# Gated cross-attention and feed-forward block: who squares the key tiles

## The chip, the cores and the metric

The kernel runs on one core of a Trainium2 chip. A core has a matrix engine (TensorE), a vector engine (VectorE), an engine for activations (ScalarE), a programmable engine (GpSimd) and one that issues transfers (SyncE). Each works through its own list of instructions in order; they wait for each other by semaphores. The metric is the device time of one execution in microseconds (us), the median of several runs.

## What is computed

The inputs are 16 batches of 512 tokens with 512 channels, a context of 120 tokens for each batch, positions, a mask and the weights. Two gated steps follow one another.

```
x = x + tanh(g_xattn) * attention(layernorm(x), ctx)     # 16 heads of 32, e / (1 + sum e), bias by distance
x = x + tanh(g_ffn)   * ffn(layernorm(x))

def ffn(x):
    xr = mu_r * x + (1 - mu_r) * x_prev                  # x_prev: the token before
    xk = mu_k * x + (1 - mu_k) * x_prev
    r  = sigmoid(xr @ W_r)
    k_act = square(relu(xk @ W_k))
    return r * (k_act @ W_v)
```

The change touches `square` in the `k_act` line.

## The kernel before

The kernel goes through the 16 batches in a loop. The attention of batch b is interleaved with the feed-forward of batch b-1, so the loop body `batch(b, ffn, last)` exists once on every engine, and in it each engine's order is written out by hand. Batch 0 has no feed-forward beside it; the batches 1 to 15 have, and the feed-forward of the last batch runs in a tail with code of its own (`tail_relu`, `tail_square`, `tail_high`, `tail_low`). Products are made to full precision by splitting each operand into a high and a low part (fp32r) and multiplying three times: high by high, high by low, low by high. Four channel tiles by three passes make 12 matmuls of 128x512 for a product.

The attention goes by token tiles t = 0 to 3 and groups of four heads g = 0 to 3. For each tile TensorE makes the scores (L589), VectorE adds the bias (L1188) and takes the row maxima (L1194), ScalarE makes the exponentials of 16 heads (`exps`, L884), VectorE the reciprocals of the sums (L1207, L1209), GpSimd normalises half a tile at a time (`normalise_probs`, L1496), TensorE transposes by groups (L683) into two banks in turn, ScalarE copies them out (`probs_out`, L891), TensorE multiplies by the values (L694), ScalarE and VectorE split the result (`attn_out` L898, `attn_low` L1213), and TensorE projects it.

The feed-forward's key step goes by channel tiles m = 0 to 3. TensorE makes a key product in one of two rotating banks. ScalarE takes it with a Relu into `relu` (`relu_out`, L932), GpSimd squares `relu` into `square` (`squares`, L1533), ScalarE rounds `square` to the high part of `xt_or_act` (`act_split`, L936), and GpSimd subtracts to get the low part (`squares_low`, L1537). `relu` and `square` are single buffers: the Relu of tile m+1 waits until square m is made (`square_ready`), and the square of tile m+1 until low part m is made (`act_low`). The first value product reads `xt_or_act` channel tile by channel tile and waits for each low part (`act_low`). Tiles 0 to 3 are worked on while the attention's tiles 0 and 1 go through softmax. Both buffers also serve as scratch for the mixing step of the odd token tiles (`diffs`, `mix_ks`), which comes later in the batch.

Of the kernel before, what the change touches and what calls it, by code (L numbers as in the profile page):

```python
# [10 lines left out]
ALU = mybir.AluOpType  # L11
ACT = mybir.ActivationFunctionType
# [31 lines left out]
def flamingo_block(nc, x, x_t, ctx_t, qpos, kpos, mask, g_xattn, g_ffn, wq, wk, wv, wo,  # L44
# [6 lines left out]
    CT = D // P  # L51
# [19 lines left out]
    with ExitStack() as stack:  # L71
        def sb(name, shape, dt=F32):
            return stack.enter_context(nc.sbuf_tensor(name, shape, dt))

        def sem(name):
            return stack.enter_context(nc.semaphore(name))
# [35 lines left out]
        relu = sb("relu", [P, S])  # L112
        square = sb("square", [P, S])
# [91 lines left out]
        read = {k: sem(f"{k}_read") for k in ("key", "gate", "value", "proj", "query", "turn2")}  # L205
# [44 lines left out]
        square_ready = sem("square_ready")  # L250
        act_high = sem("act_high")
        act_low = sem("act_low")
# [580 lines left out]
        def _(act):  # L833
# [45 lines left out]
            def exps(b, t, g):  # L879

                act.wait_ge(max_ready, (b * QT + t) * G + g + 1)
                for j in range(J):
                    head = g * J + j
                    e = act.activation(probs[:, t % 2, head, :], probs[:, t % 2, head, :], ACT.Exp,  # L884
                                       bias=neg_max[:, t % 2, head:head + 1],
                                       accum_out=sums[:, t % 2, head:head + 1])
                e.then_inc(exp_done, 1)
# [37 lines left out]
            def relu_out(b, m):  # L925
# [5 lines left out]
                    act.wait_ge(square_ready, b * CT + m)  # L931
                act.activation(relu[:], bank_of["key", m][:], ACT.Relu).then_inc(read["key"], 1)  # L932

            def act_split(b, m):
                act.wait_ge(square_ready, b * CT + m + 1)
                act.copy(xt_or_act[:, HI, m, :], square[:]).then_inc(act_high, 1)  # L936
# [27 lines left out]
            def batch(b, ffn, last):  # L964
                f = b - 1

                def feed_forward(*steps):
                    for step, n in steps:
                        if ffn:
                            step(f, n)  # L970
                        elif (step, n) in late:
                            late_out(late[step, n])

                def after(*steps):
                    if not last:
                        for step, n in steps:
                            step(b + 1, n)

                late = {(gate_out, n): LATE_USES.index(("gate", n)) for n in range(QT)}
                late.update({(relu_out, n): LATE_USES.index(("key", n)) for n in range(CT)})  # L980
                feed_forward((gate_out, 0))
                exps(b, 0, 0)
                exps(b, 0, 1)
                feed_forward((gate_out, 1))
                exps(b, 0, 2)
                exps(b, 0, 3)
                feed_forward((relu_out, 0))
                probs_out(b, 0, 0)
                probs_out(b, 0, 1)
                exps(b, 1, 0)  # L990
                feed_forward((act_split, 0), (relu_out, 1))
                exps(b, 1, 1)
                probs_out(b, 0, 2)
                probs_out(b, 0, 3)
                exps(b, 1, 2)
                feed_forward((act_split, 1))
                attn_out(b, 0)
                feed_forward((relu_out, 2))
                exps(b, 1, 3)
                feed_forward((act_split, 2))  # L1000
                exps(b, 2, 0)
                probs_out(b, 1, 0)
                probs_out(b, 1, 1)
                feed_forward((relu_out, 3))
                probs_out(b, 1, 2)
                probs_out(b, 1, 3)
                feed_forward((act_split, 3))
                exps(b, 2, 1)
                exps(b, 2, 2)
                attn_out(b, 1)  # L1010
                exps(b, 2, 3)
                after((split_x_high, 0))
                probs_out(b, 2, 0)
                after((split_x_high, 1))
                exps(b, 3, 0)
                exps(b, 3, 1)
                probs_out(b, 2, 1)
                probs_out(b, 2, 2)
                probs_out(b, 2, 3)
                feed_forward((gate_out, 2))  # L1020
                turn2_out(b, 0)
                attn_out(b, 2)
                exps(b, 3, 2)
                exps(b, 3, 3)
                probs_out(b, 3, 0)
                probs_out(b, 3, 1)
                after((split_x_high, 2))
                probs_out(b, 3, 2)
                probs_out(b, 3, 3)
                turn2_out(b, 1)  # L1030
                mix_key_high(b, 0)
                attn_out(b, 3)
                feed_forward((gate_out, 3))
                mix_gate_high(b, 0)
                after((split_x_high, 3))
                if not ffn:

                    act.wait_ge(late_done, len(LATE_USES))
                    weight(5)
                mix_key_high(b, 1)  # L1040
                if not last:
                    turn2_out(b, 2)
                    mix_gate_high(b, 1)
                    mix_key_high(b, 2)
                    turn2_out(b, 3)
                    mix_key_high(b, 3)
                    mix_gate_high(b, 2)
                else:
                    mix_gate_high(b, 1)
                    turn2_out(b, 2)  # L1050
                    mix_key_high(b, 2)
                    mix_gate_high(b, 2)
                    gate_out(b, 0, tail_bank)
                    turn2_out(b, 3)
                    gate_out(b, 1, tail_bank)
                    mix_key_high(b, 3)
                mix_gate_high(b, 3)
# [35 lines left out]
            with act.Fori(1, NB - 1) as b:  # L1093
                batch(b, True, False)
# [365 lines left out]
        def _(pool):  # L1460
# [65 lines left out]
                pool.tensor_tensor(mixed_gate[:, LO, :, tokens], diffs[t % 2][:], as_f32(mixed_gate[:, HI, :, tokens]),  # L1526
                                   ALU.subtract).then_inc(mixg_low, 1)

            def squares(b, m):
                pool.wait_ge(read["key"], b * CT + m + 1)  # L1530
                if m > 0:
                    pool.wait_ge(act_low, b * CT + m)
                pool.tensor_tensor(square[:], relu[:], relu[:], ALU.mult).then_inc(square_ready, 1)  # L1533

            def squares_low(b, m):
                pool.wait_ge(act_high, b * CT + m + 1)
                pool.tensor_tensor(xt_or_act[:, LO, m, :], square[:], as_f32(xt_or_act[:, HI, m, :]),  # L1537
# [2 lines left out]
            def batch(b, ffn, last):  # L1540
                f = b - 1

                def feed_forward(*steps):
                    if ffn:
                        for step, n in steps:
                            step(f, n)

                def after(*steps):
                    if not last:
                        for step, n in steps:  # L1550
                            if n is None:
                                step(b + 1)
                            else:
                                step(b + 1, n)

                normalise_probs(b, 0, 0)
                feed_forward((squares, 0))
                normalise_probs(b, 0, 1)
                feed_forward((squares_low, 0), (squares, 1))
                normalise_probs(b, 1, 0)  # L1560
                feed_forward((squares_low, 1), (squares, 2))
                normalise_probs(b, 1, 1)
                feed_forward((squares_low, 2), (squares, 3), (squares_low, 3))
                rstd2_of(b, 0)
                normalise_probs(b, 2, 0)
                normalise_probs(b, 2, 1)
                after((split_x_low, 0))
                normalise_probs(b, 3, 0)
                edge(b, 0)
                difference(b, 0)  # L1570
                rstd2_of(b, 1)
                normalise_probs(b, 3, 1)
                after((split_x_low, 1), (split_x_low, 2))
                edge(b, 1)
                rstd2_of(b, 2)
                after((rstd1_of, None))
                difference(b, 1)
                after((split_x_low, 3))
                if last:
                    mix_low(b, 0)  # L1580
                    mix_low(b, 1)
                edge(b, 2)
                if not last:
                    mix_low(b, 0)
                rstd2_of(b, 3)
                if not last:
                    mix_low(b, 1)
                difference(b, 2)
                edge(b, 3)
                difference(b, 3)  # L1590
                mix_low(b, 2)
                mix_low(b, 3)
# [35 lines left out]
```

## Time and profile before

| | us |
|---|---|
| median of 3 runs | 1287.36 |
| lowest, highest | 1286.8, 1287.39 |
| the profiled execution | 1286.61 |
| its span on the core | 1284.8 |
| TensorE busy | 1271.9 |
| VectorE busy | 1048.6 |
| ScalarE busy | 836.7 |
| GpSimd busy | 782.2 |

The span is what the profile's rows cover; the rest of the execution lies around it. Busy times count instructions that run, not waits. The granted clock of TensorE is at its full level throughout. In rows of the timeline the first number is the start in us from the span's start and the second the time from the start of the first to the end of the last of the instructions merged in the row; on ScalarE an instruction may start while the one before it is ending. Brackets at a row's end give idle time before it and the engine that ended it. PE is TensorE's matmul, PEld its weight load, DVE is VectorE, ACT ScalarE and POOL GpSimd.

### The profile page before, as it was taken

To read this page: it belongs to the slowest core of one execution; us is meant where nothing else is said; L and a number is where in the kernel's file an instruction comes from. 1 tells how busy PE (TensorE), PEld (TensorE's weight loads), DVE (VectorE), ACT (ScalarE), POOL (GpSimd) and SP (SyncE) were. 2 spreads that over 40 slices of the span, in tenths; PEclk is the share of its full clock that TensorE was granted. 3 is DMA by queue.
4 is the path that set the end of the run, shared out by engine and by line. 5 is a ranking of instruction groups with operands and counts; after the bars stand their busy time and mean duration, and the time that the engine had idled before them with its cause. 6 is when DMAs were issued, how large, how long until landed. Compare 5 with 4: busy or idle time off the path is not lost.

```text
span 1284.8 us, 30825 instructions
## 1 busy us (share of the span) xinstructions
PE 1271.9 (99%) x9848; PEld 1044.9 (81%) x9848; DVE 1048.6 (82%) x2834; ACT 836.7 (65%) x2868; POOL 782.2 (61%) x731
## 2 busy tenths in 40 slices
PE   8999999999999999999999999999999999999998
PEld 7888788888878888888888888888888888888887
DVE  4767797988978788888978798897879888798885
ACT  5457494875848395674939477584848667493952
POOL 0014666666666676676676766666676666676651
PEclk9999999999999999999999999999999999999999
DMA  9772314032231304123130402213140312312000
GB/s 286 211 230 73 114 36 131 8 78 86 58 98 57 106 8 116 48 59 105 50 105 24 139 8 70 94 50 105 48 115 8 100 64 59 105 50 56 10 26 33
DMA packets 75377, 103.74 MB, mean 81 GB/s; under 512 B 26960, under 2 KB 33104, under 8 KB 75344
## 3 DMA queue, kind: packets, MB, share of 16 engines
q1 hardware_dynamic: 75344, 103.31, 26.9%
q8 instruction: 19, 0.31, 0.1%
q14 instruction: 14, 0.11, 0.0%
HBM read 78.62 MB, written 24.67 MB: 80 GB/s over the span
## 4 chain that ended last, share of the span: by engine, by line
PE 97%; DVE 1%; issue 1%; POOL 0%; ACT 0%; DMA 0%; DVEq 0%; ACTq 0%; POOLq 0%
PE rotating L510 71%; PE score_bank L589 5%; PE attn_bank L694 5%; PE probs_bank L683 5%; PE attn_bank L683 4%; PE score_bank L510 4%; PE score_bank L605 2%; PE probs_bank L605 0%; DVE w_value L1132 0%; DMA probs<-in_ctx_t_dram 0%; PE probs_bank L510 0%; PE attn_bank L510 0%; DVE mix_k L1252 0%; DVE square L1252 0%; PE attn_bank L551 0%
## 5 line engine op out<-in xcount | busy, mean ns | idle before, releaser
L884 ACT ACTIVATE probs<-probs,neg_max 128x120 f32<-128x120 f32 x1024 | 390.7, 386 | 8.0 <-DVE neg_max L1194 7.0
L1496 POOL TENSOR_TENSOR probs<-probs,recip 128x960 f32<-128x960 f32 x128 | 232.5, 1816 | 177.4 <-DVE recip L1209 177.4
L1188 DVE SCALAR_TENSOR_TENSOR probs<-mask_in,score_bank 128x120 f32<-128x120 f32 x1024 | 213.7, 271 | 24.0 <-PE score_bank L589 23.9
L884 ACT ACTIVATION_READ_ACCUMULATOR probs<-probs,neg_max 128x1 f32 x1024 | 195.3, 191 | 0.0
L510 PE MATMUL rotating<-w_gate,mixed_gate 128*128 128x512 f32 x756 | 190.9, 398 | 3.2 <-DVE query_t L1173 2.5
L510 PE MATMUL rotating<-w_proj,attn_t 128*128 128x512 f32 x768 | 191.5, 398 | 0.0
L510 PE MATMUL rotating<-w_value,xt_or_act 128*128 128x512 f32 x720 | 180.1, 399 | 0.0
L510 PE MATMUL rotating<-mixed_key,w_key 128*128 128x512 f32 x720 | 178.2, 396 | 0.0
L510 PE MATMUL rotating<-xt_or_act,w_query 128*128 128x512 f32 x744 | 176.1, 392 | 0.0
L1194 DVE TENSOR_REDUCE neg_max<-probs 128x4 f32<-128x480 f32 x256 | 166.4, 650 | 7.1
L510 PEld LDWEIGHTS rotating<-w_proj,attn_t 128*128 128x128 f32 x768 | 141.6, 188 | 37.1 <-issue 5.8
L510 PEld LDWEIGHTS rotating<-w_gate,mixed_gate 128*128 128x128 f32 x756 | 137.2, 188 | 31.2 <-issue 3.8
L510 PEld LDWEIGHTS rotating<-xt_or_act,w_query 128*128 128x128 f32 x744 | 138.5, 188 | 29.2 <-issue 0.3
L510 PEld LDWEIGHTS rotating<-mixed_key,w_key 128*128 128x128 f32 x720 | 131.7, 188 | 28.6 <-issue 3.2
L510 PEld LDWEIGHTS rotating<-w_value,xt_or_act 128*128 128x128 f32 x720 | 130.7, 188 | 27.8 <-issue 3.0
L916 ACT CAST mixed_key<-mix_k 128x512 fp32r<-128x512 f32 x32 | 20.4, 639 | 140.6 <-DVE mix_k L1252 140.6
L1482 POOL TENSOR_TENSOR xt_or_act<-xt_raw,xt_or_act 128x512 fp32r<-128x512 f32 x60 | 84.1, 1403 | 42.5 <-ACT xt_or_act L877 41.4
L891 ACT COPY probs_t<-attn_bank 120x512 f32<-120x512 f32 x128 | 75.3, 588 | 44.3 <-PE attn_bank L683 43.9
L891 ACT COPY probs_t<-probs_bank 120x512 f32<-120x512 f32 x128 | 74.2, 580 | 43.6 <-PE probs_bank L683 43.4
L1537 POOL TENSOR_TENSOR xt_or_act<-square,xt_or_act 128x512 fp32r<-128x512 f32 x60 | 77.2, 1287 | 38.7 <-ACT xt_or_act L936 38.7
L1173 DVE SCALAR_TENSOR_TENSOR query_t<-rotating,rstd_row 128x512 f32<-128x512 f32 x62 | 66.1, 1066 | 40.2 <-PE rotating L510 40.2
L1533 POOL TENSOR_TENSOR square<-relu 128x512 f32<-128x512 f32 x60 | 62.4, 1041 | 35.7 <-ACT relu L932 31.3
(129 smaller groups left out, 2165.2 us busy)
## 6 DMA issues: line engine op xcount, KB each, us to landing
x_again<-in_x_dram SPq DMA_DIRECT2D x64, 256.0 KB, 3.6
xt_raw<-in_x_t_dram SPq DMA_DIRECT2D x16, 1024.0 KB, 6.9
xs<-in_x_dram SPq DMA_DIRECT2D x64, 256.0 KB, 3.2
out_dram<-gated SPq DMA_DIRECT2D x64, 256.0 KB, 2.0
rstd_row<-rstd_scratch SPq DMA_DIRECT2D x16, 256.0 KB, 5.2
value_scratch<-gated SPq DMA_DIRECT2D x16, 240.0 KB, 3.8
mask_in<-in_mask_dram SPq DMA_DIRECT2D x16, 240.0 KB, 2.7
keys_t<-key_scratch SPq DMA_DIRECT2D x16, 240.0 KB, 5.8
```

Of the source, the lines that this page charges most:

```text
L510: mm = pe.matmul(bank, stationary(a, c), moving(b, c), start=(i == 0), stop=(i == MATMULS - 1))
L589: mm = pe.matmul(score_banks[j][:, g * NK:(g + 1) * NK], query_t[rows, g, t * P:(t + 1) * P], keys_t[rows, g, :], start=True, stop=True)
L683: mm = pe.transpose(bank[0:NK, j * P:(j + 1) * P], probs[:, t % 2, g * J + j, :], ident[:])
L694: mm = pe.matmul(attn_bank[j * HD:(j + 1) * HD, g * P:(g + 1) * P], values[:, head * HD:(head + 1) * HD], probs_t[:, g, j, :], start=True, ...
L884: e = act.activation(probs[:, t % 2, head, :], probs[:, t % 2, head, :], ACT.Exp, bias=neg_max[:, t % 2, head:head + 1], accum_out=sums[:, ...
L891: act.copy(probs_t[:, g], turned_bank[g % 2][0:NK, :].rearrange("k (j q) -> k j q", j=J))\
L1173: dve.scalar_tensor_tensor(out=by_tile(query_t[:, m, :]), in0=by_tile(banks["query", m][:]), scalar=SCALE, in1=rstd_row[:].rearrange("a (p ...
L1188: z = dve.scalar_tensor_tensor(out=probs[:, t % 2, head, :], in0=neg_dist[:, t, :], scalar=SLOPES[head], in1=score_banks[j][:, g * NK:(g + ...
L1194: dve.tensor_reduce(neg_max[:, t % 2, g * J:(g + 1) * J], probs[:, t % 2, g * J:(g + 1) * J, :], AX.X, ALU.max, negate=True).then_inc(max_ ...
L1482: pool.tensor_tensor(xt_or_act[:, LO, :, tokens], xt_raw[:, :, tokens], as_f32(xt_or_act[:, HI, :, tokens]), ALU.subtract).then_inc(xt_low, 1)
L1496: pool.tensor_tensor(part, part, recip[:, t % 2, heads].unsqueeze(2).to_broadcast((P, H // 2, NK)), ALU.mult)\
L1537: pool.tensor_tensor(xt_or_act[:, LO, m, :], square[:], as_f32(xt_or_act[:, HI, m, :]), ALU.subtract).then_inc(act_low, 1)
```

## The change

The function `squares` moves from GpSimd's program to ScalarE's. In place of a multiplication of `relu` by itself it is an activation with the function Square. It keeps its semaphores. On ScalarE it is put directly ahead of `act_split` of the same tile, in all of the batches with a feed-forward; GpSimd's list is the same without its four squares. The tail after the last batch, where VectorE squares, is left as it is.

```
@@ ScalarE
+            def squares(b, m):
+                act.wait_ge(read["key"], b * CT + m + 1)
+                if m > 0:
+                    act.wait_ge(act_low, b * CT + m)
+                act.activation(square[:], relu[:], ACT.Square).then_inc(square_ready, 1)
...
                 exps(b, 1, 0)
-                feed_forward((act_split, 0), (relu_out, 1))
+                feed_forward((squares, 0), (act_split, 0), (relu_out, 1))
...
                 exps(b, 1, 2)
-                feed_forward((act_split, 1))
+                feed_forward((squares, 1), (act_split, 1))
                 attn_out(b, 0)
                 feed_forward((relu_out, 2))
                 exps(b, 1, 3)
-                feed_forward((act_split, 2))
+                feed_forward((squares, 2), (act_split, 2))
...
                 probs_out(b, 1, 3)
-                feed_forward((act_split, 3))
+                feed_forward((squares, 3), (act_split, 3))
@@ GpSimd
-            def squares(b, m):
-                pool.wait_ge(read["key"], b * CT + m + 1)
-                if m > 0:
-                    pool.wait_ge(act_low, b * CT + m)
-                pool.tensor_tensor(square[:], relu[:], relu[:], ALU.mult).then_inc(square_ready, 1)
...
                 normalise_probs(b, 0, 0)
-                feed_forward((squares, 0))
                 normalise_probs(b, 0, 1)
-                feed_forward((squares_low, 0), (squares, 1))
+                feed_forward((squares_low, 0))
                 normalise_probs(b, 1, 0)
-                feed_forward((squares_low, 1), (squares, 2))
+                feed_forward((squares_low, 1))
                 normalise_probs(b, 1, 1)
-                feed_forward((squares_low, 2), (squares, 3), (squares_low, 3))
+                feed_forward((squares_low, 2), (squares_low, 3))
```

ScalarE's list in a batch with feed-forward, before, from the exponentials of token tile 1 on (the names left of the arrow are written, right of it read; the last number is the tile's size, in brackets the semaphores waited for):

```order
L884 ACTIVATE probs,sums<-probs,neg_max 128x120 [waits max_ready]
L884 ACTIVATE probs,sums<-probs,neg_max 128x120 x3
L936 CAST xt_or_act<-square 128x512 [waits square_ready]
L932 ACTIVATE relu<-rotating 128x512 [waits square_ready,key_done]
L884 ACTIVATE probs,sums<-probs,neg_max 128x120 [waits max_ready]
L884 ACTIVATE probs,sums<-probs,neg_max 128x120 x3
L891 COPY probs_t<-probs_bank 120x512 [waits probs_turned]
L891 COPY probs_t<-attn_bank 120x512 [waits probs_turned]
L884 ACTIVATE probs,sums<-probs,neg_max 128x120 [waits max_ready]
L884 ACTIVATE probs,sums<-probs,neg_max 128x120 x3
L936 CAST xt_or_act<-square 128x512 [waits square_ready]
L898 CAST attn_t<-attn_bank 128x512 [waits proj_done,attn_done]
```

And the same stretch of the changed kernel:

```order
L938 ACTIVATE square<-relu 128x512 [waits key_read]
L942 CAST xt_or_act<-square 128x512 [waits square_ready]
L932 ACTIVATE relu<-rotating 128x512 [waits square_ready,key_done]
L884 ACTIVATE probs,sums<-probs,neg_max 128x120 [waits max_ready]
L884 ACTIVATE probs,sums<-probs,neg_max 128x120 x3
L891 COPY probs_t<-probs_bank 120x512 [waits probs_turned]
L891 COPY probs_t<-attn_bank 120x512 [waits probs_turned]
L884 ACTIVATE probs,sums<-probs,neg_max 128x120 [waits max_ready]
L884 ACTIVATE probs,sums<-probs,neg_max 128x120 x3
L938 ACTIVATE square<-relu 128x512 [waits act_low,key_read]
L942 CAST xt_or_act<-square 128x512 [waits square_ready]
L898 CAST attn_t<-attn_bank 128x512 [waits proj_done,attn_done]
```

Each split has a square ahead of it, and everything behind stands in the same order. The lines behind the new function have moved down by six (L936 is L942). ScalarE's list holds one table load, its first instruction, before and after.

GpSimd's list in the same batch, before:

```order
L1496 TENSOR_TENSOR probs<-probs,recip 128x960 [waits recip_ready]
L1533 TENSOR_TENSOR square<-relu 128x512 [waits key_read]
L1496 TENSOR_TENSOR probs<-probs,recip 128x960 [waits recip_ready]
L1537 TENSOR_TENSOR xt_or_act<-square,xt_or_act 128x512 [waits act_high]
L1533 TENSOR_TENSOR square<-relu 128x512 [waits act_low,key_read]
L1496 TENSOR_TENSOR probs<-probs,recip 128x960 [waits recip_ready]
L1537 TENSOR_TENSOR xt_or_act<-square,xt_or_act 128x512 [waits act_high]
```

And of the changed kernel:

```order
L1502 TENSOR_TENSOR probs<-probs,recip 128x960 [waits recip_ready] x2
L1537 TENSOR_TENSOR xt_or_act<-square,xt_or_act 128x512 [waits act_high]
L1502 TENSOR_TENSOR probs<-probs,recip 128x960 [waits recip_ready]
L1537 TENSOR_TENSOR xt_or_act<-square,xt_or_act 128x512 [waits act_high]
L1502 TENSOR_TENSOR probs<-probs,recip 128x960 [waits recip_ready]
```

The squares are gone, the low parts stand behind the same normalisations as before. The low part's line is L1537 in both kernels, since six lines came in above it and six went out.

## Rows read from the trace of the kernel before

**Rows 1.** The page: busy us (share) xinstructions by engine, and the chain's shares.

```profile
PE 1271.9 (99%) x9848; PEld 1044.9 (81%) x9848; DVE 1048.6 (82%) x2834; ACT 836.7 (65%) x2868; POOL 782.2 (61%) x731
...
PE 97%; DVE 1%; issue 1%; POOL 0%; ACT 0%; DMA 0%; DVEq 0%; ACTq 0%; POOLq 0%
```

**Rows 2.** TensorE's waits in the whole span: us in total, times, longest us.

```profile
PE score_bank L510 <- DVE mixed_key L1127: 5.6, 1, 5.6
...
PE rotating L510 <- POOL mixed_gate L1526: 0.7, 1, 0.7
```

**Rows 3.** Instructions by line: duration ns min/median/max, first and last start us, forms.

```profile
L932 ACT ACTIVATE relu<-rotating x60: 571/589/604, 164.7 to 1211.1; 128x512 f32<-128x512 f32 x60
...
L1533 POOL TENSOR_TENSOR square<-relu x60: 1039/1041/1042, 165.4 to 1211.8; 128x512 f32<-128x512 f32 x60
...
L837 ACT ACT_TABLE_LOAD  x1: 1283/1283/1283, 0.7 to 0.7; - x1
```

**Rows 4.** Timeline of ScalarE, a steady batch: start us, us, instruction, [idle <-releaser].

```profile
682.55 0.40 ACT L884 ACTIVATE probs<-probs,neg_max 128x120 f32<-128x120 f32 x1 [0.40 <-DVE neg_max L1194]
...
684.08 0.60 ACT L936 CAST xt_or_act<-square 128x512 fp32r<-128x512 f32 x1
...
686.60 0.57 ACT L891 COPY probs_t<-probs_bank 120x512 f32<-120x512 f32 x1
687.19 0.59 ACT L891 COPY probs_t<-attn_bank 120x512 f32<-120x512 f32 x1
...
689.71 0.58 ACT L898 CAST attn_t<-attn_bank 128x512 fp32r<-128x512 f32 x1
...
690.68 0.39 ACT L884 ACTIVATE probs<-probs,neg_max 128x120 f32<-128x120 f32 x1
...
692.39 0.62 ACT L936 CAST xt_or_act<-square 128x512 fp32r<-128x512 f32 x1
...
694.45 0.56 ACT L891 COPY probs_t<-probs_bank 120x512 f32<-120x512 f32 x1
695.23 0.59 ACT L891 COPY probs_t<-attn_bank 120x512 f32<-120x512 f32 x1 [0.22 <-PE attn_bank L683]
695.71 0.60 ACT L932 ACTIVATE relu<-rotating 128x512 f32<-128x512 f32 x1
696.91 0.59 ACT L891 COPY probs_t<-probs_bank 120x512 f32<-120x512 f32 x1 [0.59 <-PE probs_bank L683]
...
697.87 0.63 ACT L936 CAST xt_or_act<-square 128x512 fp32r<-128x512 f32 x1
```

**Rows 5.** Timeline of GpSimd, same batch.

```profile
680.66 1.04 POOL L1533 TENSOR_TENSOR square<-relu 128x512 f32<-128x512 f32 x1 [1.77 <-ACT relu L932]
...
698.58 1.29 POOL L1537 TENSOR_TENSOR xt_or_act<-square,xt_or_act 128x512 fp32r<-128x512 f32 x1 [1.15 <-ACT xt_or_act L936]
```

**Rows 6.** Timeline of VectorE, same batch.

```profile
681.39 0.34 DVE L1207 TENSOR_SCALAR sums<-sums 128x8 f32<-128x8 f32 x1
...
692.56 0.17 DVE L1207 TENSOR_SCALAR sums<-sums 128x8 f32<-128x8 f32 x1
```

**Rows 7.** Timeline of TensorE, same batch; merged rows of 12 and 18 products.

```profile
691.72 3.03 PE L510 MATMUL rotating<-w_proj,attn_t 128*128 128x512 f32 x12
...
699.63 4.38 PE L510 MATMUL rotating<-w_value,xt_or_act 128*128 128x512 f32 x18
```

**Rows 8.** Timeline of setup and tail: how soon a waiting instruction starts.

```profile
13.28 0.19 ACT L1065 ACTIVATE gates<-gates_in 128x2 f32<-128x2 f32 x1
13.50 0.20 ACT L1067 ACTIVATE half_gate<-gates 128x1 f32<-128x1 f32 x1
...
1256.93 1.32 POOL L1526 TENSOR_TENSOR mixed_gate<-diff,mixed_gate 128x512 fp32r<-128x512 f32 x1
...
1258.39 2.97 PE L510 MATMUL rotating<-w_gate,mixed_gate 128*128 128x512 f32 x12 [0.73 <-POOL mixed_gate L1526]
```

## The prediction

> **What bounds the kernel now.** I read the page's busy shares and its chain first [rows 1], then TensorE's waits [rows 2], and then one batch instruction by instruction [rows 4 to 7]. The reader is to see three things. TensorE is busy 1271.9 of 1284.8 us, and 97% of the chain is TensorE [rows 1]. Its waits for others are three in the whole span, 5.6 us the longest and 0.7 us the shortest, the third between them [rows 2]; the first lies in the setup and the last in the tail, so in the steady batches TensorE never stands still. What TensorE gains nowhere it can still lose: a steady batch repeats every 73.6 us or so (the 60 Relus start from 164.7 to 1211.1, 14 batches and 15.7 us apart) [rows 3]; ScalarE is busy 65% on average [rows 1], but not evenly. From 682.55 to 697.87, where the four key tiles are turned into activations, ScalarE's instructions stand nearly back to back [rows 4]. That is just the stretch into which the change puts four more.
>
> **What is removed.** 60 multiplications on GpSimd (four in each of the 15 batches that carry a feed-forward), 1041 ns each [rows 3]: 62 us of GpSimd time. GpSimd is not what TensorE waits for, so by itself this is worth nothing. One side effect reaches ScalarE: VectorE's small operation on the sums took 0.34 us at 681.39 and 0.17 us at 692.56 [rows 6]. The first one lay beside the multiplication of 680.66 to 681.70 [rows 5] and ended 0.03 us after it. With the multiplication gone I take 0.15 us off VectorE's path to the row maxima, for which the exponentials of 682.55 wait.
>
> **What is added.** 60 Square activations of 128x512 f32 on ScalarE. No row shows a Square. The nearest one is the Relu of the same size and types on the same engine, 589 ns, from 571 to 604 [rows 3]. The step also changes form: the split that follows must wait for the square on its own engine. Without a wait ScalarE starts its next instruction before the last one has ended, 0.11 us early (the relu of 695.71 follows a copy that started at 695.23 and lasts 0.59 us) [rows 4]. With a wait on its own result it does not: the two small activations in the setup stand 13.28 + 0.19 to 13.50, 0.03 us apart [rows 8]. So a square costs s = 0.60 + 0.05 = **0.65 us** of ScalarE's time. Bounds: 0.57 + 0.03 = 0.60 from below; from above 0.63 + 0.08 = 0.71, with the split of 697.87 in place of the Relu and the 0.08 us from its end, 698.50, to GpSimd's start at 698.58 [rows 4, 5]. I take 0.65 since Relu is the nearer row.
>
> The Trainium skill, "ScalarE: Activation LUTs", section "What ACT_TABLE_LOAD costs", gives 186 ns + 0.833 ns per element for an ACTIVATE with immediate operands, which would be 0.61 us here and an s of 0.66 by its estimate; each pointer operand adds 93 ns, and if the zero bias is one, s would be 0.75 and the sum some 6 us more. The Relu's 589 ns agrees with the form without a pointer.
>
> **What lies on the path: a ledger of how late ScalarE is.** I follow the batch of 680 to 703 us. Late means against the same instruction of before.
> - At 682.55: 0.15 us early (above).
> - Square 0 goes in at 684.08, in front of the split that stands there: +0.65, so 0.50 late.
> - The copy of 687.19 was waiting; ScalarE was free at 686.60 + 0.48 = 687.08. The gap takes 0.11: 0.39 late.
> - Square 1, ahead of the second split: 1.04 late. The copy of the attention bank (689.71) is as late, and then VectorE and TensorE's projection behind it.
> - Before the split of 692.39 stood a gap for GpSimd's square: 690.68 + 1.53 (four exponentials, as 682.55 to 684.08) = 692.21, so 0.18. It goes, and square 2 comes: 1.04 - 0.18 + 0.65 = 1.51.
> - Before the copy of 695.23: free at 694.45 + 0.48 = 694.93, gap 0.30: 1.21 late.
> - Before the copy of 696.91: free at 695.71 + 0.48 = 696.19, gap 0.72: 0.49 late.
> - Square 3, ahead of the last split: 0.49 + 0.65 = **1.14 us late** at what was 697.87 [rows 4].
>
> In short 4 x 0.65 - (0.11 + 0.18 + 0.30 + 0.72) - 0.15 = 1.14.
>
> The last low part on GpSimd follows that split at once and ended at 698.58 + 1.29 = 699.87 [rows 5]; with the change at 701.01. The value product of TensorE reads it as its fourth channel tile. Its second half starts at 699.63, 18 products in 4.38 us, 0.24 each [rows 7], and three of them belong to the third tile: the fourth tile's first product starts at about 700.35, its weights one product earlier, at 700.11. From the end of a GpSimd instruction to the product waiting for it went 1256.93 + 1.32 = 1258.25 to 1258.39, 0.14 us [rows 8]. So before, 700.35 - 0.14 - 699.87 = 0.34 us were left (0.12 if the weights count), and now TensorE is late by 1.14 - 0.34 = 0.80 to 1.14 - 0.12 = 1.02. I take the middle, **0.9 us per batch**. Stops of TensorE on the way (attention over the values, the projection of 691.72, the transposes of the second tile) are smaller parts of the same delay, because each later product is measured from its old place; they do not add.
>
> Nothing gives it back, since TensorE has no idle time later in the batch. The other engines start the next batch from TensorE's scores, so their lateness ends there. 15 batches x 0.9 = **13.4 us**. Against the profiled execution's own time, 1286.61 us (span 1284.8 and 1.8 around it), that is 1300.0; the median of the runs shown is 0.75 us higher, so **1300.8 us**. With s = 0.60 and 0.34 us of slack the loss is 0.60 x 15 = 9 us, 1296; with s = 0.71 and 0.12 it is 1.26 x 15 = 19 us, 1306.
>
> The new waits themselves: square 2 waits for the low part 1, on GpSimd behind the second tile's first probabilities, and square 3 for low part 2, behind the second half. By the ledger square 2 could start at 692.21 + 1.04 = 693.25, and low part 1 is ready about a microsecond before; square 3 has more. Behind a waiting square stand exponentials and the probability copies, for which TensorE waits, so had this cover gone, its whole length would come on top.
>
> **Rivals.**
> A, *absorbed*: the gaps and the slack take all. That needs 4s - 1.46 below 0.12 to 0.34, so s at 0.40 to 0.45, less than even an unwaited 0.48 of its neighbours. Time 1287 to 1289. Against it are all the 512-wide rows of ScalarE. Chance 0.07.
> B, *faster*: GpSimd's multiplication holds up VectorE at 681.39 [rows 5, 6]; if such holds, not ScalarE, set the values' start, freeing GpSimd would let TensorE start earlier. It decides only where TensorE waits for GpSimd or VectorE, and outside the first 60 us that was 0.7 us in the tail plus at most the 2.5 us of the middle row [rows 2]. Time 1284 to 1287. Chance 0.03.
> C, *the gaps don't absorb*: the 0.30 and 0.72 us were waits for TensorE's transposes, and when these are late too (they need copies that are late) the gaps stay. Then the delay is 4 x 0.65 - 0.15 - 0.11 - 0.18 = 2.16, less 0.24 of slack, 1.9 per batch: 1287.4 + 29 = 1316. For it: the transposes of the second tile do need the copy of 694.45, which becomes 1.5 us late. Against: by the ledger TensorE is only about 0.5 late there. A part of it would end near 1308. Chance 0.15, of which 0.08 beyond 1310.
> D, *table loads*: Square sits in another table than Exp. One load took 1283 ns [rows 3], two for each square would be 60 x 2 x 1.28 = 154 us, some 1440. The new ScalarE order has a single load, the first row of the program, as before. Chance 0.01. The Trainium skill, "ScalarE: Activation LUTs", section "Table sets: the hidden batching unit", names a switch of sets as the cost to fear and lists no square beside exp and tanh; the 1283 ns of the row is its figure for a load.
>
> **How the numbers follow.** The forecast has 0.74, A 0.07, B 0.03, C 0.15, D 0.01. The range is 1293 to 1310: the forecast's own 1296 to 1306, a little of A's side if the slack was larger than I read it, and half of C. A measurement tells about 0.2% from no change, 2.6 us. Slower by more than that: 0.90 (forecast, C and D); same: 0.07 (A); faster: 0.03 (B).
>
> **What would show it.** In the profile after: Square rows of about 0.60 us, each split 0.03 to 0.08 us behind its square; ScalarE busy about 36 us more, GpSimd 62 less; the gap before the split of the third tile gone; new waits of TensorE for ScalarE's copies, VectorE's part of the attention and GpSimd's last low part, with the value product's as the last of each batch; a batch of 74.5 us in place of 73.6. The prediction is wrong if TensorE's waits stay at three (A), if the value product isn't among those that wait, or if the Square takes over 0.7 us.

## The result and the profile after

The changed kernel takes **1297.64 us** (median of 4 runs, 1297.31 to 1297.81); the kernel before beside it takes 1287.38 us (4 runs). The ratio is 1.0084, with a 95% interval from 1.0072 to 1.0096: 10.3 us slower, where 13.4 were forecast.

The page after first, the lines that answer to [rows 1]; the second line is the chain's shares by engine.

```profile
PE 1279.4 (99%) x9848; PEld 1044.2 (81%) x9848; DVE 1046.7 (81%) x2834; ACT 868.8 (67%) x2928; POOL 720.2 (56%) x671
...
PE 84%; ACT 8%; DVE 4%; issue 2%; POOL 0%; DMA 0%; ACTq 0%; DVEq 0%; POOLq 0%
```

ScalarE has 32 us more and GpSimd 62 less. For ScalarE 36 were forecast; the instructions that stood behind a gap now overlap with the one ahead of them. TensorE's share of the chain fell from 97% to 84%, ScalarE's rose from nothing to 8% and VectorE's from 1% to 4%: the path now leaves TensorE in each batch. TensorE's busy time rose by 7.5 us with the same 9848 matmuls, since a product whose weights come late is shown as busy. The stop itself must be read from the waits. The kernel after, what TensorE and its weight loads waited for, in us in total, times, longest us (to be read beside [rows 2]):

```profile
PE score_bank L510 <- DVE mixed_key L1133: 5.7, 1, 5.7
PE rotating L510 <- DVE attn_t L1219: 2.9, 14, 0.2
PE rotating L510 <- DVE query_t L1179: 2.5, 1, 2.5
PE rotating L510 <- POOL mixed_gate L1532: 0.7, 1, 0.7
```

```profile
PEld rotating L510 <- ACT relu L932: 6.2, 15, 0.4
PEld rotating L510 <- POOL xt_or_act L1537: 6.1, 15, 0.4
```

Two waits are new, once in each of the 15 batches. One is the projection's, on the attention's split (the load's wait is put down to the Relu, which ended at 695.86 + 0.60 = 696.46, TensorE's own to VectorE's half, which came last, at 695.99 + 0.69 = 696.68). The other is the value product's, on the last low part. The prediction named both. It named a third, for ScalarE's copies, and no such wait is in the list.

The new instruction and its follower, by line, in ns min/median/max:

```profile
L938 ACT ACTIVATE square<-relu x60: 615/627/647, 167.9 to 1223.6; 128x512 f32<-128x512 f32 x60
```

```profile
L942 ACT CAST xt_or_act<-square x60: 617/620/622, 168.6 to 1224.3; 128x512 fp32r<-128x512 f32 x60
```

And the timeline of ScalarE after, in the batch that answers to [rows 4]. Its first Relu starts at 684.64 where that of before starts at 680.00, so 4.64 is to be taken off for a comparison.

```profile
687.02 0.40 ACT L884 ACTIVATE probs<-probs,neg_max 128x120 f32<-128x120 f32 x1 [0.22 <-DVE neg_max L1200]
...
688.55 0.61 ACT L938 ACTIVATE square<-relu 128x512 f32<-128x512 f32 x1
...
689.20 0.62 ACT L942 CAST xt_or_act<-square 128x512 fp32r<-128x512 f32 x1
...
692.19 0.58 ACT L891 COPY probs_t<-attn_bank 120x512 f32<-120x512 f32 x1
...
695.38 0.58 ACT L898 CAST attn_t<-attn_bank 128x512 fp32r<-128x512 f32 x1
...
698.52 0.62 ACT L942 CAST xt_or_act<-square 128x512 fp32r<-128x512 f32 x1
...
701.03 0.57 ACT L891 COPY probs_t<-attn_bank 120x512 f32<-120x512 f32 x1
...
702.01 0.59 ACT L891 COPY probs_t<-probs_bank 120x512 f32<-120x512 f32 x1
...
702.97 0.64 ACT L938 ACTIVATE square<-relu 128x512 f32<-128x512 f32 x1
703.65 0.62 ACT L942 CAST xt_or_act<-square 128x512 fp32r<-128x512 f32 x1
```

The ledger, forecast and read (us late against before, after taking off 4.64):

| instruction | forecast | read |
|---|---|---|
| exponentials of 682.55 | -0.15 | -0.17 |
| first split | 0.50 | 0.48 |
| copy of 687.19 | 0.39 | 0.36 |
| attention copy of 689.71 | 1.04 | 1.03 |
| third split | 1.51 | 1.49 |
| copy of 695.23 | 1.21 | 1.16 |
| copy of 696.91 | 0.49 | 0.46 |
| last split | 1.14 | 1.14 |

TensorE of the kernel after in the same batch, the rows that answer to [rows 7], and the transpose that follows the value products:

```profile
696.83 3.03 PE L510 MATMUL rotating<-w_proj,attn_t 128*128 128x512 f32 x12 [0.21 <-DVE attn_t L1219]
...
704.75 4.63 PE L510 MATMUL rotating<-w_value,xt_or_act 128*128 128x512 f32 x18
709.22 0.60 PE L683 MATMUL probs_bank<-ident,probs 128*120 128x128 f32 x4
```

The projection is 696.83 - 4.64 - 691.72 = 0.47 us late and the value product's second half starts 0.48 late. Its 18 products take 4.63 in place of 4.38 us [rows 7], so it ends 0.73 late. That is 11 us in 15 batches, against 10.3 in the medians and 10.7 in the spans of the two profiled executions. Of the 0.47 at the projection 0.21 is shown as idle; the rest, 0.26, and the 0.25 at the value product are about the 7.5 us by which TensorE's busy time rose (15 x 0.51 = 7.7).

### The profile page after: what moved, and what is told of

Same layout as the page of the kernel before. It is cut to its first block, busy times and chain, and to the rows that moved or that the text cites. A ratio compares the mean times of both kernels' runs of the same rounds, so it can differ in the third digit from the quotient of the medians.

```text
span 1295.5 us, 30825 instructions
## 1 busy us (share of the span) xinstructions
PE 1279.4 (99%) x9848; PEld 1044.2 (81%) x9848; DVE 1046.7 (81%) x2834; ACT 868.8 (67%) x2928; POOL 720.2 (56%) x671
## 4 chain that ended last, share of the span: by engine, by line
PE 84%; ACT 8%; DVE 4%; issue 2%; POOL 0%; DMA 0%; ACTq 0%; DVEq 0%; POOLq 0%
PE rotating L510 63%; ACT probs L884 5%; PE score_bank L589 4%; PE attn_bank L694 4%; PE score_bank L510 4%; PE attn_bank L683 3%; PE probs_bank L683 3%; PE score_bank L605 2%; ACT square L938 1%; DVE probs L1194 1%; DVE attn_t L1219 1%; ACT probs_t L891 1%; DVE neg_max L1200 1%; ACT relu L932 1%; ACT attn_t L898 1%
## 5 line engine op out<-in xcount | busy, mean ns | idle before, releaser
L510 PE MATMUL rotating<-w_value,xt_or_act 128*128 128x512 f32 x720 | 184.2, 402 | 0.0
L1537 POOL TENSOR_TENSOR xt_or_act<-square,xt_or_act 128x512 fp32r<-128x512 f32 x60 | 77.1, 1285 | 87.7 <-ACT xt_or_act L942 87.7
L683 PE MATMUL probs_bank<-ident,probs 128*120 128x128 f32 x512 | 79.3, 277 | 0.0
```

The source lines that it names most:

```text
L510: mm = pe.matmul(bank, stationary(a, c), moving(b, c), start=(i == 0), stop=(i == MATMULS - 1))
L683: mm = pe.transpose(bank[0:NK, j * P:(j + 1) * P], probs[:, t % 2, g * J + j, :], ident[:])
```

## The experiments

Each kernel was timed in turns with the kernel before on the same chip. The edits are shown against the kernel after, unless the text says otherwise; a square that is taken off ScalarE stands in GpSimd's list again, where it was before. The questions: are the two stops of TensorE one delay (contained) or two losses (additive); do the gaps of ScalarE really absorb; how large is the slack at the value product; is it the place of the squares or their work that costs; and what was VectorE's lead worth.

### One stop removed

```
-                feed_forward((squares, 1), (act_split, 1))
                 attn_out(b, 0)
+                feed_forward((squares, 1), (act_split, 1))
```

> The changed kernel with one thing moved: ScalarE copies the attention bank (attn_out of tile 0) ahead of the second square and split instead of behind them. My theory (contained): TensorE's loss of a batch is the lateness of the last low part less the slack at the value product, 1.13 - 0.41 = 0.72 us; the projection's stop (0.47) is inside it. Then the projection's stop goes and the value product's stop grows by as much, and the time stays at about 1297.6 us (+10). Rival (additive): the two stops are losses of their own, 0.47 + 0.25; without the first one the loss is 0.25 x 15 = 4 us, 1291.

Measured: 1297.96 us against 1287.06, ratio 1.0084 (1.0071 to 1.0098), 10.9 us. The wait on the attention's split is gone, and the time is that of the changed kernel. Its timeline of TensorE, where 4.95 is to be taken off (its first Relu starts at 684.95):

```profile
696.80 3.06 PE L510 MATMUL rotating<-w_proj,attn_t 128*128 128x512 f32 x12
...
705.05 4.62 PE L510 MATMUL rotating<-w_value,xt_or_act 128*128 128x512 f32 x18
709.50 0.60 PE L683 MATMUL probs_bank<-ident,probs 128*120 128x128 f32 x4
```

ScalarE's half of the attention's split is early now and VectorE's ends at 696.40, so the projection starts only 0.13 late, 0.05 behind the end of the third Relu (696.16 + 0.59 = 696.75), which empties the bank that the projection writes:

```profile
696.16 0.59 ACT L932 ACTIVATE relu<-rotating 128x512 f32<-128x512 f32 x1
```

The value product's second half is 0.47 late all the same. The weight loads of the transposes before it wait for ScalarE's late copies, which they did not in the kernel after:

```profile
PEld probs_bank L683 <- ACT probs_t L891: 3.7, 14, 0.3
```

The value product's own wait stays: it ends at 709.50 - 4.95 = 704.55 against 703.86, 0.7 late as before. The stops are one delay that TensorE meets wherever it first asks. Additive expected 4 us; the measured 10.9 is 7 us away from it, and the interval's lower end, 9.1, still 5.

### The same squares in ScalarE's gaps

```
-                feed_forward((relu_out, 0))
+                feed_forward((relu_out, 0), (squares, 0))
...
-                feed_forward((squares, 0), (act_split, 0), (relu_out, 1))
+                feed_forward((act_split, 0), (relu_out, 1))
...
                 probs_out(b, 0, 2)
+                feed_forward((squares, 1))
                 probs_out(b, 0, 3)
                 exps(b, 1, 2)
-                feed_forward((squares, 1), (act_split, 1))
+                feed_forward((act_split, 1))
...
-                feed_forward((relu_out, 3))
+                feed_forward((relu_out, 3), (squares, 3))
                 probs_out(b, 1, 2)
                 probs_out(b, 1, 3)
-                feed_forward((squares, 3), (act_split, 3))
+                feed_forward((act_split, 3))
```

> All four squares stay on ScalarE, but they stand where ScalarE was idle: square 0 right behind the first Relu, square 3 right behind the last Relu, square 1 between the third and the fourth probability copy, so that three of the four splits no longer wait for their own engine; square 2 stays. Ledger of before: last split late by about -0.17 + 0.50 - 0.11 + 0.66 - 0.18 - 0.30 + 0.64 - 0.72 = 0.3 us, under the slack of 0.41 at the value product, and the attention copy late by 0.2 to 0.3, about its slack of 0.23. My theory: the loss nearly goes, 1287 to 1289 us. Rival (the 34 us of work that ScalarE gets are what costs, wherever they stand): 1296 to 1298.

Measured: 1287.52 us (11 runs) against 1287.06, ratio 1.0002 (0.9993 to 1.0011), no difference that can be told. All 60 squares are on ScalarE. In its timeline of ScalarE the squares of tiles 0, 1 and 3 have other instructions between them and their splits:

```profile
681.11 0.57 ACT L932 ACTIVATE relu<-rotating 128x512 f32<-128x512 f32 x1
681.71 0.63 ACT L938 ACTIVATE square<-relu 128x512 f32<-128x512 f32 x1
682.25 0.57 ACT L891 COPY probs_t<-probs_bank 120x512 f32<-120x512 f32 x1
...
687.98 0.63 ACT L938 ACTIVATE square<-relu 128x512 f32<-128x512 f32 x1
688.51 0.57 ACT L891 COPY probs_t<-attn_bank 120x512 f32<-120x512 f32 x1
...
699.26 0.63 ACT L942 CAST xt_or_act<-square 128x512 fp32r<-128x512 f32 x1
```

A square that nobody waits for on its own engine takes 0.53 to 0.54 us of ScalarE instead of 0.65 to 0.68. Square 0 stands behind the Relu that it reads and waits for it: 0.60 us lie between the two starts where an unwaited instruction would follow after 0.48 or 0.49. That costs the same 0.12, but here a gap takes it. The last split is 699.26 - 1.11 - 697.87 = 0.28 late, the forecast of 0.3, and within the slack. The two new waits of TensorE are gone from the list. So it is the place, not the work.

### Only the squares of tiles 0 and 1

The squares of tiles 2 and 3 are GpSimd's multiplications as before.

```
-                feed_forward((squares, 2), (act_split, 2))
+                feed_forward((act_split, 2))
...
-                feed_forward((squares, 3), (act_split, 3))
+                feed_forward((act_split, 3))
```

> Only the squares of tiles 0 and 1 are on ScalarE, those of tiles 2 and 3 on GpSimd as before. Attention copy late as in the full change: the projection stops 0.47 us. After that the gaps of 0.30 and 0.72 take ScalarE's own lateness, and the last low part is late by no more than TensorE. My theory: 0.47 x 15 = 7 us, 1294.4. Rival (each square costs its share, half of 10.3): 1292.5.

Measured: 1295.24 us against 1287.06, ratio 1.0066 (1.0053 to 1.008), 8.2 us, where 7 were expected and half of the whole would be 5. The trace has the projection's stop alone, at the expected size (first Relu at 683.51, so 3.51 off: 0.47 late), and it stays 0.46 at the transpose after the value products:

```profile
695.70 3.03 PE L510 MATMUL rotating<-w_proj,attn_t 128*128 128x512 f32 x12 [0.20 <-DVE attn_t L1219]
...
707.83 0.60 PE L683 MATMUL probs_bank<-ident,probs 128*120 128x128 f32 x4
```

The two squares alone have two thirds of the loss or more, not a half (the interval is 6.8 to 10.3 us, a half is 5). The microsecond over 7 lies inside the interval, and this trace doesn't show where it would be.

### Only the square of tile 3

```
-                feed_forward((squares, 0), (act_split, 0), (relu_out, 1))
+                feed_forward((act_split, 0), (relu_out, 1))
...
-                feed_forward((squares, 1), (act_split, 1))
+                feed_forward((act_split, 1))
...
-                feed_forward((squares, 2), (act_split, 2))
+                feed_forward((act_split, 2))
```

> Only the square of tile 3 is on ScalarE, directly ahead of its split. Ledger: nothing is late until there, then 0.66 us; less the slack of 0.41 read from the changed kernel's trace that is 0.25 a batch, 3.7 us, 1291.1. With the slack as I recorded it in the prediction (0.12 to 0.34) it would be 0.32 to 0.54, 5 to 8 us, 1292 to 1295. Rival (shares of 10.3 by square): 2.6 us, 1290.

Measured: 1291.44 us against 1287.06, ratio 1.0033 (1.0022 to 1.0043), 4.4 us. That is nearest to the slack of 0.41; the larger of the recorded slacks, 0.34, gives 5 and isn't excluded, the smaller one (8 us) is. The rival's 2.6 us lies just under the interval (2.8 to 5.5), so the time alone hardly excludes it. The trace says more: the 18 products take 0.26 us more than the 4.38 of before, which in 15 batches is 3.9 us.

```profile
703.54 4.64 PE L510 MATMUL rotating<-w_value,xt_or_act 128*128 128x512 f32 x18
```

### Only the squares of tiles 2 and 3

```
-                feed_forward((squares, 0), (act_split, 0), (relu_out, 1))
+                feed_forward((act_split, 0), (relu_out, 1))
...
-                feed_forward((squares, 1), (act_split, 1))
+                feed_forward((act_split, 1))
```

> Only the squares of tiles 2 and 3 are on ScalarE. Ledger: square 2 makes the third split 0.66 - 0.18 = 0.48 us late, the gap of 0.30 leaves 0.18, the gap of 0.72 leaves nothing, square 3 makes 0.66. My theory (the gaps swallow square 2 whole): same as with square 3 alone, 0.25 x 15 = 3.7 us, 1291. Rival (no gap absorbs): 1.3 - 0.41 = 0.9 a batch, 13 us, 1301; rival (shares by square): 5 us, 1292.5.

Measured: 1290.92 us against 1287.25, ratio 1.0028 (1.0018 to 1.0039), 3.7 us: no more than square 3 alone. The gaps swallow square 2 whole. The rival without gaps, 13 us, is excluded; that of equal shares, 5 us, lies at the interval's upper end (2.3 to 5.0), and the rows speak against it. In its timeline of ScalarE (1.07 off) the copy that stood at 695.23 is 0.14 late, and the next one waits for TensorE again and is on time:

```profile
696.44 0.58 ACT L891 COPY probs_t<-attn_bank 120x512 f32<-120x512 f32 x1
696.92 0.59 ACT L932 ACTIVATE relu<-rotating 128x512 f32<-128x512 f32 x1
697.97 0.59 ACT L891 COPY probs_t<-probs_bank 120x512 f32<-120x512 f32 x1 [0.46 <-PE probs_bank L683]
```

### The slack at the value product

The kernel before, with one copy that no result uses ahead of the last split:

```
+            def filler(b, n):
+                act.copy(mix_k[:], mix_k[:])
...
-                feed_forward((act_split, 3))
+                feed_forward((filler, 0), (act_split, 3))
```

> The kernel before, squares on GpSimd, with one extra ScalarE copy of 128x512 (a buffer onto itself, no result uses it) directly ahead of the last split of each batch. It makes the last low part late by 0.49 to 0.52 us and touches nothing else, so it measures the slack at the value product. Slack of 0.41 (read from the traces): 0.1 a batch, 1 to 2 us, 1288.9. Slack of 0.12 to 0.34 (as recorded in the prediction): 0.16 to 0.39 a batch, 2.4 to 6 us, 1290 to 1293.

Measured: 1288.56 us against 1287.25, ratio 1.001 (1.0001 to 1.0019), 1.3 us. With two of them, the second one on `diff`:

```
-                feed_forward((act_split, 3))
+                feed_forward((filler, 0), (filler, 1), (act_split, 3))
```

> The kernel before with two such copies ahead of the last split of each batch, about 1.0 us. Slack of 0.41: 0.59 to 0.61 a batch, 9 us, 1296.3. Slack of 0.12 to 0.34: 0.66 to 0.9 a batch, 10 to 13.5 us, 1297 to 1301. The difference from the kernel with one copy should be 15 x 0.49 to 0.51 = 7.5 us in either case, if nothing else waits first.

Measured: 1297.26 us against 1287.25, ratio 1.0079 (1.0065 to 1.0093), 10.0 us. Two rows of its ScalarE timeline give the price of a copy, 0.52 us; below them TensorE's wait at the value product:

```profile
703.19 0.63 ACT L935 COPY mix_k<-mix_k 128x512 f32<-128x512 f32 x1
703.71 0.63 ACT L935 COPY diff<-diff 128x512 f32<-128x512 f32 x1
```

```profile
704.96 0.96 PE L510 MATMUL rotating<-w_value,xt_or_act 128*128 128x512 f32 x3
706.28 3.69 PE L510 MATMUL rotating<-w_value,xt_or_act 128*128 128x512 f32 x15 [0.36 <-POOL xt_or_act L1540]
```

And in the kernel with one copy the same 18 products in one row:

```profile
700.47 4.51 PE L510 MATMUL rotating<-w_value,xt_or_act 128*128 128x512 f32 x18
```

By the times, one copy costs 1.3/15 = 0.09 us a batch, so the slack is 0.52 - 0.09 = 0.43 (0.36 to 0.51 by the interval); two cost 0.67, so 1.04 - 0.67 = 0.37 (0.24 to 0.48). The run with one copy excludes the prediction's 0.12 to 0.34; the one with two does not exclude its upper part. The traces are sharper. With one copy the products take 4.51 - 4.38 = 0.13 more, which leaves 0.39 of 0.52; with two they take 706.28 + 3.69 - 704.96 = 5.01, 0.63 more, which leaves 0.41 of 1.04. The kernel after gave 0.41 too. The second copy costs 8.7 us more in time where 7.8 would be its own; 0.9 us, not explained, within the intervals.

### GpSimd's first multiplication given back

```
+            def filler(b, m):
+                pool.wait_ge(read["key"], b * CT + m + 1)
+                pool.tensor_tensor(mix_k[:], mix_k[:], mix_k[:], ALU.mult)
...
                 normalise_probs(b, 0, 0)
+                feed_forward((filler, 0))
                 normalise_probs(b, 0, 1)
```

> The changed kernel with a multiplication of the same size given back to GpSimd where the first square stood (on a buffer of its own that is idle there, no result uses it). If VectorE's operation on the sums is held up by it as before, ScalarE's exponentials start 0.15 to 0.17 us later, and since ScalarE is back to back from there this goes through to TensorE: 15 x 0.16 = 2.4 us more, 1300. Rival (the lead of VectorE was worth nothing): 1297.6.

Measured: 1300.93 us against 1287.25, ratio 1.0108 (1.0093 to 1.0124). That is 13.7 us over before, against 10.3 for the change alone: 3.4 us for the extra multiplication, where 2.4 were expected. A difference of two such measurements is uncertain by some 2.5 us, so its size is better read from the trace. Its VectorE and GpSimd timelines show the hold-up itself:

```profile
687.87 0.34 DVE L1213 TENSOR_SCALAR sums<-sums 128x8 f32<-128x8 f32 x1
```

```profile
687.14 1.04 POOL L1537 TENSOR_TENSOR mix_k<-mix_k 128x512 f32<-128x512 f32 x1 [1.77 <-ACT relu L932]
```

and in the kernel after, without it, the same VectorE operation is back at 0.17:

```profile
686.03 0.17 DVE L1213 TENSOR_SCALAR sums<-sums 128x8 f32<-128x8 f32 x1
```

The exponentials behind it have lost their lead, and the value products end later (6.49 is to be taken off: its first Relu starts at 686.49):

```profile
689.04 0.40 ACT L884 ACTIVATE probs<-probs,neg_max 128x120 f32<-128x120 f32 x1 [0.40 <-DVE neg_max L1200]
```

```profile
711.25 0.60 PE L683 MATMUL probs_bank<-ident,probs 128*120 128x128 f32 x4
```

The exponentials stand at 689.04 - 6.49 = 682.55, where they stood before, and TensorE is 711.25 - 6.49 - 703.86 = 0.90 late against 0.72 in the kernel after. So the change had a gain in it of 0.18 us a batch, some 2.7 us, and the loss is net of that.

## Why the prediction was right, and which term was off

**What bounds the kernel, and the direction**: right. TensorE had nothing to win and lost time at two of the three places named, with 15 stops each; the third, ScalarE's copies, makes it wait only in the run with the attention's copy moved. The sum had a slip: 15 x 0.9 is 13.5, not 13.4.

**The price of a square**, 0.65 us: right; read 0.65 to 0.68. It is made otherwise than I put it: the instruction takes 627 ns, not 600, and the split starts 0.03 to 0.04 us behind its end, not 0.05. The two errors, 0.03 and 0.01, have opposite signs; that the price came out so near is in part luck. Relu takes 593 ns in the same trace. The Trainium skill's estimate by size ("ScalarE: Activation LUTs", "What ACT_TABLE_LOAD costs"), 0.61 without a pointer operand, is within 0.02 of the row; the 0.71 with one is not what the row shows.

**The ledger**: right within 0.05 us at every point. The run with squares 2 and 3, no slower than square 3 alone, shows that the gaps absorb, and the run with the squares in the gaps that the same work costs nothing there.

**The slack at the value product**: the term that was mis-sized. I took 0.24 us, the middle of 0.12 and 0.34; it is 0.39 to 0.41 in the traces. Two parts of it were wrong. I let the product wait 0.14 us for a GpSimd result, by a row of the tail [rows 8]. In the batches the wait ends sooner: GpSimd's last low part ends at 704.35 + 1.28 = 705.63, and the load starts at 705.68. In the kernel after, GpSimd's row and then the weight loads:

```profile
704.35 1.28 POOL L1537 TENSOR_TENSOR xt_or_act<-square,xt_or_act 128x512 fp32r<-128x512 f32 x1 [2.84 <-ACT xt_or_act L942]
```

```profile
704.75 0.53 PEld L510 LDWEIGHTS rotating<-w_value,xt_or_act 128*128 128x128 f32 x3 [0.20 <-issue]
705.68 0.30 PEld L510 LDWEIGHTS rotating<-w_value,xt_or_act 128*128 128x128 f32 x2 [0.40 <-POOL xt_or_act L1537]
```

With two copies ahead of the split, where the matmul itself stood still, it too resumed 0.05 behind GpSimd's end (704.94 + 1.29 = 706.23, and the product at 706.28):

```profile
704.94 1.29 POOL L1540 TENSOR_TENSOR xt_or_act<-square,xt_or_act 128x512 fp32r<-128x512 f32 x1 [2.18 <-ACT xt_or_act L939]
```

Why it was 0.14 in the tail stays open. And I thought the weights might be needed a whole product earlier. They are loaded early if they can be, but the 0.40 us in which the load stood idle cost the products only 4.63 - 4.38 = 0.25: the load has a lead, and TensorE loses only what exceeds it. With both put right the prediction's own sum gives 700.35 - 0.05 - 699.87 = 0.43, close to what was measured. With 0.41 in place of 0.24 the loss is (1.14 - 0.41) x 15 = 11 us, against 10.3 measured.

**VectorE's lead of 0.15**: right, 0.17 read, and it goes when the multiplication is given back.

**The rivals.** A (absorbed) needed a square under 0.45 us; with the true slack, under 0.47. It was 0.66. It is what happens in another order, with the squares in the gaps. B (faster) had the hold-up right, some 2.7 us, but ScalarE's lateness outweighs it. C (the gaps don't absorb) fell with the ledger read, 1.14 at the last split and not 2.16, and with squares 2 and 3 alone, 3.7 us and not 13. D (table loads): one load in the whole program after, as before, and none between Exp and Square in any of the 60:

```profile
L837 ACT ACT_TABLE_LOAD  x1: 1283/1283/1283, 0.7 to 0.7; - x1
```

The Trainium skill, "ScalarE: Activation LUTs", "Table sets: the hidden batching unit", doesn't list Square beside Exp and Tanh (its row names only some of the set's functions); this case shows that a kernel with all three runs on one load.

## What to carry to other kernels

The same work moved to an engine with 35% idle time cost 10 us or nothing here, by where in the order it stood. To tell which, write down how late the engine gets at each instruction, take off each gap that waits for another engine, and compare with the slack of the first consumer on the bounding engine. Put a new instruction where the engine waited for someone else. Directly ahead of the instruction that reads its result it costs more, 0.12 us each time here, unless a gap takes that. Stops of the bounding engine that come from one late chain are one loss, as large as the lateness in excess of slack at the worst place: with the first stop removed nothing was won, and with the last one gone (squares 0 and 1 alone) 8.2 of 10.3 us stayed.

## What the runs showed of the hardware

- ScalarE's 128x512 f32 instructions with their source in SBUF took 0.61 to 0.63 us (medians of Square, the splits, the filler copies), those that read PSUM 0.58 to 0.60 (Relu, the attention copy, and the probability copies, which are 120x512). I had taken Relu's time for the square.
- The end of a ScalarE instruction to the start of the one that waits for it on ScalarE itself was 0.03 to 0.04 us, where without a wait the next starts 0.09 to 0.11 us before the end. Waiting for one's own result costs 0.12 to 0.14 us.
- TensorE's weight load resumed 0.05 us behind the end of GpSimd's instruction in the batches; in the tail the product came 0.14 behind it. A load that stood idle 0.40 us made the products 0.25 us longer.
- A VectorE operation of 128x8 elements was held until GpSimd's multiplication ended, in the kernel before and again when a multiplication was put back (0.34 against 0.17 us). The second such operation of the batch was held too, in the kernel before: it ended at 686.76 + 0.50 = 687.26, the second multiplication at 686.20 + 1.04 = 687.24.

```profile
686.76 0.50 DVE L1207 TENSOR_SCALAR sums<-sums 128x8 f32<-128x8 f32 x1
```

```profile
686.20 1.04 POOL L1533 TENSOR_TENSOR square<-relu 128x512 f32<-128x512 f32 x1
```
